# Attention on one core: pair additions of E given to VectorE by a comparison of two modelled clocks

## What is computed

```python
Q = split_heads(Xn @ Wq + bq)            # 16 heads of 32
K = split_heads(Xn @ Wk + bk)
V = split_heads(Xn @ Wv + bv)
scores = jnp.einsum('bhqd,bhkd->bhqk', Q, K) / jnp.sqrt(jnp.float32(D_HEAD))
scores = jnp.where(causal, scores, jnp.float32(-jnp.inf))
A = jax.nn.softmax(scores, axis=-1)
AV = jnp.einsum('bhqk,bhkd->bhqd', A, V)
return AV @ Wo + bo
```

## Time and profile before

| | us |
|---|---|
| three runs, median (lowest to highest) | 2539.11 (2538.65 to 2540.96) |
| the profiled execution's own time | 2538.51 |
| its span, first to last instruction | 2536.7 |
| TensorE busy | 2455.5 |
| VectorE, ScalarE, GpSimd busy | 1776.0, 1479.5, 1534.2 |
| granted TensorE clock over the span | 0.996 |

### The profile page before, as it was taken

One profiled execution on the slowest core, in us unless ns is written; L12 is line 12 of the kernel. 1 busy time (PEld: TensorE's weight loads), 2 busy tenths in 40 slices (PEclk: granted clock), 3 DMA queues, 4 the chain that ended last, 5 costly groups with the idle time before them and its releaser, 6 DMA issues.

```text
span 2536.7 us, 40214 instructions
## 1 busy us (share of the span) xinstructions
PE 2455.5 (97%) x14559; PEld 1076.0 (42%) x14559; DVE 1776.0 (70%) x3020; ACT 1479.5 (58%) x2829; POOL 1534.2 (60%) x1596
## 2 busy tenths in 40 slices
PE   5899999999999999999999999999999999999998
PEld 3444444444443343333344434334333444444443
DVE  7966666667659685958586696958577766666665
ACT  6666666665225656566622356565674466666665
POOL 3466677765325767677342267676774466776775
PEclk9999999999999999999999999999999999999999
DMA  2012211121122020200231322020005201111111
GB/s 68 17 34 84 92 51 50 51 100 50 51 60 62 6 53 6 52 6 19 87 132 34 74 49 47 12 54 6 19 5 192 82 17 51 50 51 51 51 34 51
DMA packets 78022, 130.62 MB, mean 51 GB/s; under 512 B 19551, under 2 KB 24698, under 8 KB 77694
## 3 DMA queue, kind: packets, MB, share of 16 engines
q1 hardware_dynamic: 77822, 128.05, 16.4%
HBM read 68.23 MB, written 31.46 MB: 39 GB/s over the span
## 4 chain that ended last, share of the span: by engine, by line
PE 77%; DVE 8%; POOL 6%; ACT 2%; issue 2%; SPq 1%; DMA 0%; POOLq 0%; DVEq 0%; ACTq 0%
PE pp L97 58%; PE ps L97 17%; POOL sb L106 5%; DVE sb L118 3%; DVE sb L112 2%; ACT sb L103 2%; SPq L139 1%; PE ps L100 1%; POOL sb L109 1%; DVE sb L106 1%; DMA sb<-sb 0%; PE pp L100 0%; DVE sb L115 0%; DVE sb L109 0%; DVE sb L136 0%
## 5 line engine op out<-in xcount | busy, mean ns | idle before, releaser
L97 PE MATMUL pp<-sb,sb 128*128 128x512 f16 (+9 forms) x11228 | 2055.8, 420 | 25.2 <-DVE sb L112 14.2
L106 POOL TENSOR_TENSOR sb<-sb,sb 128x512 f32<-128x512 f32 (+6 forms) x1345 | 1480.9, 1129 | 971.4 <-ACT sb L103 316.4
L97 PEld LDWEIGHTS pp<-sb,sb 128*128 128x128 f16 (+3 forms) x11228 | 776.2, 101 | 1053.8 <-issue 234.4
L97 PE MATMUL ps<-sb,sb 128*128 128x512 f16 (+6 forms) x2788 | 722.8, 348 | 24.6 <-DVE sb L112 15.3
L103 ACT ACTIVATE sb<-pp 128x512 f32<-128x512 f32 (+6 forms) x1019 | 516.1, 548 | 287.8 <-PE pp L97 272.7
L118 DVE TENSOR_REDUCE sb<-pp 128x1 f32<-128x512 f32 (+2 forms) x720 | 453.3, 667 | 191.4 <-PE pp L97 188.9
L103 ACT ACTIVATE sb<-sb 128x512 f16<-128x512 f32 (+4 forms) x513 | 325.9, 649 | 366.9 <-DVE sb L112 307.1
L112 DVE SCALAR_TENSOR_TENSOR sb<-pp,sb,sb 128x512 f32<-128x512 f32 x447 | 324.4, 746 | 150.9 <-PE pp L97 136.0
L112 DVE SCALAR_TENSOR_TENSOR sb<-ps,sb,sb 128x512 f32<-128x512 f32 x437 | 318.1, 747 | 156.1 <-PE ps L97 129.7
L97 PEld LDWEIGHTS ps<-sb,sb 128*128 128x128 f16 (+2 forms) x2788 | 255.5, 98 | 345.9 <-DVE sb L118 36.2
L103 ACT ACTIVATE sb<-ps 128x512 f32<-128x512 f32 (+5 forms) x489 | 269.1, 557 | 152.6 <-PE ps L97 121.3
(11 more groups left out here) (29 smaller groups left out, 373.8 us busy)
## 6 DMA issues: line engine op xcount, KB each, us to landing
sb<-sb SPq DMA_DIRECT2D x144, 128.0 KB, 2.4
sb<-L_attn_X SPq DMA_DIRECT2D x64, 256.0 KB, 3.5
sb<-xa SPq DMA_DIRECT2D x64, 256.0 KB, 4.2
sb<-xc SPq DMA_DIRECT2D x64, 256.0 KB, 3.5
xa<-sb SPq DMA_DIRECT2D x32, 256.0 KB, 2.0
xc<-sb SPq DMA_DIRECT2D x32, 256.0 KB, 4.3
out<-sb SPq DMA_DIRECT2D x32, 256.0 KB, 2.0
sb<-sb SPq DMA_DIRECT2D x48, 96.0 KB, 2.2
```

The source lines that it names most:

```text
L97: return self.e.matmul(*a, **k) if self.e else self
L106: return self.e.tensor_tensor(*a, **k) if self.e else self
```

## The change

Three numbers of the planner are changed. The first is the one named in the title: an odd step goes to VectorE if its modelled clock, with the addition done there, would end more than 1000 ns ahead of GpSimd's. The other two are a weight on VectorE's lead in the time at which "stay" is a candidate, and how many scores TensorE may run ahead when no maxima are left.

```diff
-            if ready and 4 * n + j < 4 * m + 8 + (7 if wide else 3):
+            if ready and 4 * n + j < 4 * m + 8 + (6 if wide else 3):
...
-                cand.append((begin + (300.000000 - 0.200000 * min(max(dve - pe, 0), 2000) - 0.000000 * min(max(act - pe, 0), 2000)
+                cand.append((begin + (300.000000 - 0.210000 * min(max(dve - pe, 0), 2000) - 0.000000 * min(max(act - pe, 0), 2000)
...
-                      if late and n >= late or max(dve, start) + 1.04 * work + 1000000000.000000 < max(pool, start) + 2.117 * work:
+                      if late and n >= late or max(dve, start) + 1.04 * work + 1000.000000 < max(pool, start) + 2.117 * work:
```

## The result

| | before | the change |
|---|---|---|
| median of 15 runs each, us | 2538.24 | 2545.25 |
| lowest to highest | 2536.61 to 2542.23 | 2542.96 to 2548.38 |
| span of the profiled execution | 2536.7 | 2543.5 |

The ratio is 1.0026, with a 95% interval of 1.0018 to 1.0034: 7.0 us slower by the medians, 4.6 to 8.6 by the interval. I had forecast +2.6 us, and a range that ended at 2545.0; the median lies 0.25 us past its end.

What follows compares the result with a forecast made beforehand. TensorE's stream of products was taken as the bound. 2538.51 - 0.6 + 1.6 + 1.4 + 0.2 = 2541.1 us for one execution; the median, 0.6 higher, was forecast at 2541.7, range 2538.0 to 2545.0.

Steps and rivals of the forecast that it cites:

- The bound, and the work moved: In both attentions TensorE's products bound; additions moved to VectorE, 33 us more a batch, cost 0 in the qt = 3 tiles.
- What it can give: In the attentions TensorE's one wait for GpSimd, 0.3 us a batch, goes: -0.6 us, bound -1.4.
- The other two numbers ... 0: The weight and the cap on scores only shift scores by a place or two: 0.
- The first loss: the row's copy: At step 129 the row's copy comes behind Wo's split and TensorE waits: 0.8 us a batch, +1.6 us.
- the sum: 2538.51 us with all terms added gives 2541.1 for one execution; as a median 2541.7, +2.6 us.
- The second loss: step 145's addition: In the last tile it falls behind "invert" and collides with GpSimd's "level": 0.7 us a batch, +1.4 us, bounds 0 and +2.2.
- The last row: Tile (3, 3) starts later, its row's copy having four exponentials in front: +0.1 us a batch, +0.2 us.
- It cancels: Rival: both losses hide under waits already at step 129 and before step 144: 2538.7 us, chance 0.20.
- The row and the copies decide: Rival: ScalarE's backlog makes the last row 1.3 us late and both losses larger: 2547.7 us, chance 0.10.
- The lock everywhere: Rival: each moved addition collides with one of GpSimd's, so totals start late: 2545.3 us, chance 0.04.
- The gain: Rival: VectorE frees E's buffers earlier and all 3.5 us of waits for ScalarE go: 2531.5 us, chance 0.03.

Runs made afterwards that it cites:

- e2: The change with its threshold constant back at 1e9, so only the other two numbers differ from before: 2537.77 us, ratio to before 0.9996.
- e6: The change with row (3, 2) ahead of step 129's scores and the three "invert" pieces behind weigh 145: 2538.61 us, ratio to before 1.0003.
- e3: The change with row (3, 2) put ahead of step 129's scores again: 2539.97 us, ratio to before 1.0011.
- e7: The change with Wo's four ScalarE split pairs put one each behind the first score of steps 129 to 132: 2540.46 us, ratio to before 1.0008.
- e8: Before with the threshold of 1000 alone, and Wo's four split pairs spread over steps 129 to 132: 2539.49 us, ratio to before 1.0007.
- e1: Before with the threshold of 1000 alone, the other two numbers as they were: 2538.11 us, ratio to before 1.0002.
- e4: The change with the three "invert" pieces moved behind weigh 145, so step 145's addition comes first: 2540.29 us, ratio to before 1.0007.
- e9: The change with the planner's ScalarE clock charged 1280 ns for each Wo split pair: 2531.16 us, ratio to before 0.9974.
- e10: Before with the planner's ScalarE clock charged 1280 ns for each Wo split pair, nothing else: 2532.61 us, ratio to before 0.9981.
- e5: The change itself measured once more, in a later series: 2543.89 us, ratio to before 1.0022.

## Why the prediction was right or wrong

**The bound, and the work moved.** Right: TensorE bounds, VectorE's 33 us a batch lie beside it (50.00, 52.00 and 51.00 us busy in the three windows), the counts of busy time came as said, and no wait for a reduction appeared there.

**What it can give: -0.6 us, bound -1.4.** Mis-sized. The direction was right, and the 0.64 us of idle time in the first window did go, but the account gives 3.4 us for both attentions. I took as the bound the idle time that three windows show, 153 of 487 us. Looking further would not have helped: from weigh 23 to 127 TensorE is idle for 0.89 and 0.90 us in the two attentions of before and 0.16 in each of the change, so 1.5 us of the 3.4. The error is to take shown idle time for a bound. The last of a run of products is shown for 0.38 us where the pitch is 0.22, so a wait shows 0.16 us short, and a shorter one not at all. Three waits of 0.19 to 0.29 us went in each attention; with 6 x 0.16 = 1.0 us more they make 2.5 of the 3.4, by this estimate, and waits too short to be seen can hold the rest, which no run shows. (A part of each stretch's stall is only what my subtraction leaves of the products' own overhead; it is the same in both kernels, so the differences stand.) And "The other two numbers ... 0" was wrong: alone they gain 2.3 us there (12.2 to 9.9), e2.

**The first loss: the row's copy, +1.6 us.** As a wait it was right to the tenth: 3.0 against 2.2 us where the clock is full, three larger waits "that sum to about 3 us", a 32x512 copy behind the pairs. But the copy is only the last of these waits. e6, with the copy ahead, waits 3.4 us, so a row moved behind the pairs is a place where TensorE waits and not a loss by itself. Where the step failed is the sentence ahead of it: "unless the busy time itself changes, which it should not: the same products are issued". The count of products was the same, and their speed was not. Step 129 lost 6.1 us, and its rows explain it: 0.36 and 0.8 us more waiting (2.56 and 3.0 against 2.2), and 3.4 and 1.7 us by the clock, 6.3 in all. This term is missing from the sum and from the rivals, though I wrote what would show it: TensorE's busy time in the attentions off by more than 1 us. The other runs bear it out. The granted clock, which comes with each run's time, is in the mean 0.9941 over 26 runs of the change and 0.9959 over 89 of before: 0.0018 x 2540 = 4.6 us. In e3, e6, e7 and e8, 44 runs, it is 0.9960. In e1, e2 and e4 it lies between, at 0.9952, 0.9949 and 0.9948. The mean takes in falls at other places too (in the profiled executions one at 805 to 815 in the change and one at 1483 to 1493 in before, 0.83 each), so it says how much is lost and not where.

**The second loss: step 145's addition, +1.4 us.** The mechanism was right in each part (the collision of 1.0 us, GpSimd's "level" at 2.18, TensorE's wait for L106), the size low. The wait is 1.13 us an attention, not 0.7: I had worked out 0.9 and taken off a part that the exponentials might hide, and they hid nothing. The rows show 2.3 us for both (1.13 and 1.12), and e4's account 2.6 (5.7 to 3.1). The Trainium skill's page "SBUF — State Buffer", section "SBUF: two separate sides", has a VectorE instruction with two SBUF inputs and a GpSimd instruction that reads SBUF hold each other off for a whole instruction; the trace agrees, 5.69 us for four additions and 2.18 us for "level", where 4.72 and 1.28 are undisturbed. In e4, GpSimd and then VectorE, "level" starts first and is not held up, and the two additions beside it take 3.00 us and not 2.36:

```profile
1226.53 1.29 POOL L106 TENSOR_TENSOR sb<-sb,sb 128x512 f32<-128x512 f32 x1 [7.47 <-DVE sb L136]
...
1227.03 3.00 DVE L106 TENSOR_TENSOR sb<-sb,sb 128x1024 f32<-128x1024 f32 x2 [0.58 <-PE pp L97]
```

Of the last microsecond of the last tile's 3.6, a third is the last row's (below); the rest stays unattributed.

**The last row: +0.2 us.** Nearly right: TensorE waits 0.47 us for it in each attention, where it waited 0.38 in the first and 0.22 in the second, so +0.34 for both.

**The sum, by the account:** -3.4 for the moves and the two numbers, +1.2 for the waits at step 129, +5.1 for the clock, +3.6 for the last tile: 6.5 us, against 6.3 by the account's total and 7.0 by the medians. Without the clock, and with the wait of 0.8 us then seen in both attentions, it would be -3.4 + 1.6 + 3.6 = +1.8. That the forecast of +2.6 lies near this is luck: two errors cancel, a gain and a last tile both taken too small.

**The rivals.** "It cancels" is out: both losses were there in full. "The row and the copies decide" has nearly the right time and the wrong cause: the last row was not late, and the copy's wait not larger than forecast. "The lock everywhere" is out: VectorE's additions of 1024 columns have a mean of 1253 ns now against 1308. The gain is out for this list; e9 and e10 show that one of nearly its size lay in the kernel, in the uncounted pairs, which this change does not touch.

**What stays open** is why the clock falls at step 129 in the change. In the profiled executions of the change, e4 and e5 it fell there in 6 of 6 attentions; in e3, e6, e7 and e8 in 1 of 8; in before, e1 and e2 in 2 of 6. The sum of the waits does not decide it: e6 and e8 wait 3.4 us there at full clock. Nor does a single long one: the longest is 1.2 us in both the change and e6. That the row's place has to do with it is shown by the runs with the row first (e3 and e6, 22 runs, 0.9960 in the mean) against those with the change's order and the pairs together (the change and e4, 37 runs, 0.9943); by what path is not.

## What to carry to other kernels

A planner's clock is only as good as the pieces it counts: 5 us of uncharged work on ScalarE gave a list that waited behind it, and charging it gave 6.2 us together with the change that had lost 7.0, and 4.7 without it. Complete a planner's costs before judging one of its rules: neither part of this change lost anything measurable alone, and together they lost where the uncounted work stands. And when TensorE bounds a kernel, compare the granted clock and the count of products in short windows, not busy time alone: at 0.76 and 1.00, 71 and 95 products filled the same 11.7 us. Nor is shown idle time a bound on what a better order can give: 1.8 us were shown where 3.4 were gained.

## What the runs showed of the hardware

TensorE's granted clock fell to its lower level with no wait longer than 1.22 us ahead of it. TensorE is busy for 97% of the program, but not there: here are the windows of the change before, in and behind the lower stretch, of the first attention and then of the second.

```profile
1165.00:1171.50 6.50, 4.49 (x34) 1.30 (x27) 3.45 (x7) 5.19 (x12) 5.38 (x6) 1.00 0.00 0
1171.50:1178.50 7.00, 6.45 (x34) 2.39 (x34) 3.27 (x5) 3.00 (x7) 5.75 (x6) 0.51 0.06 16
1178.50:1185.00 6.50, 6.50 (x56) 2.68 (x53) 5.52 (x10) 3.99 (x10) 1.69 (x4) 1.00 0.01 1
...
1846.00:1854.00 8.00, 5.43 (x45) 2.01 (x43) 4.29 (x8) 6.64 (x14) 6.48 (x7) 1.00 0.01 2
1854.00:1858.00 4.00, 3.56 (x16) 1.28 (x20) 2.55 (x5) 1.72 (x5) 4.00 (x5) 0.57 0.09 25
1858.00:1864.00 6.00, 6.00 (x56) 2.08 (x48) 4.58 (x9) 2.96 (x8) 2.52 (x5) 1.00 0.00 1
```

Ahead of the fall TensorE was idle for 2.01 us in three waits (0.62, 0.17 and 1.22) in both. In the first attention the clock fell right behind the third; in the second it fell some 1.6 us later, during the fourth wait, and was up again after half as long. So one execution, with the same products and the same waits ahead, has 0.76 and 0.88 over 14 us, and e5 has the same two numbers; e6 and e8, with 3.4 us of waits, kept the full clock in all four attentions. The lower clock cost 3.4 and 1.7 us, where the waits had grown by 0.36 and 0.8, and it hid a part of the next wait (0.55 us against 0.99 for the same copy). So a thinned place in the stream is not priced by its idle time.
